# Self-attention of a decoder layer: float32r scores on stacks built inside SBUF, and projections interleaved with the exponentials

## The reference

```python
def attn(x, w_q, w_k, w_v, w_o):                      # 4 batches, 512 tokens, 16 heads of 16
    q, k, v = x @ w_q.T, x @ w_k.T, x @ w_v.T         # reshaped to heads
    scores = einsum('bqhd,bkhd->bhqk', q, k) * 16 ** -0.5
    out = einsum('bhqk,bkhd->bqhd', softmax(scores), v)
    return out.reshape(B, S, 256) @ w_o.T
x = layernorm(x + attn(x, ...))
x = layernorm(x + xattn(x, ctx, ...))                 # the same with keys and values from the context
x = layernorm(x + ffn(x, ...))                        # softmax router, top 2 of 8 experts, exact gelu
```

## Time and profile before

| | us |
|---|---|
| median of 3 runs (885.6 to 890.35) | 889.31 |
| profiled execution | 889.74 |
| its span, first to last instruction | 888.0 |
| front, to the first exp tile | 141 |
| self-attention, to the last PV group | 183.4 |
| the rest | 563.6 |

### The profile page before, as it was taken

How to read it: one execution, slowest core, us unless ns; L and a number is a source line. 1 busy time by engine, 2 the same in 40 slices (tenths; PEclk the granted TensorE clock), 3 DMA queues, 4 the chain that set the end, 5 groups by cost and what they waited for, 6 DMA issues and landing times.

```text
span 888.0 us, 13256 instructions
## 1 busy us (share of the span) xinstructions
PE 686.3 (77%) x4099; PEld 449.1 (51%) x4100; DVE 349.9 (39%) x750; ACT 285.8 (32%) x501; POOL 212.3 (24%) x265
## 2 busy tenths in 40 slices
PE   7572266999999986764677862099999999999980
PEld 3230111322222245541213652089999999999970
DVE  2252344888888546653443875000000000000004
ACT  3220133767666643332354211011111111111112
POOL 1020100111111122112111067213333333333322
PEclk9876786999999999886689995599999999999995
DMA  6999992000001430858713722356666566656615
GB/s 207 129 170 169 141 151 32 3 1 1 1 1 44 136 53 37 134 82 130 98 53 101 250 77 50 105 161 180 175 169 177 167 173 180 174 174 175 170 45 189
DMA packets 75777, 103.61 MB, mean 117 GB/s; under 512 B 15044, under 2 KB 60637, under 8 KB 75742
## 3 DMA queue, kind: packets, MB, share of 16 engines
q1 hardware_dynamic: 63006, 90.53, 45.0%
q0 software_dynamic: 8512, 8.44, 5.8%
q10 hardware_dynamic: 4224, 4.19, 1.7%
HBM read 82.95 MB, written 21.40 MB: 118 GB/s over the span
## 4 chain that ended last, share of the span: by engine, by line
PE 64%; DMA 14%; DVE 7%; SPq 5%; POOL 4%; issue 3%; ACT 2%; DVEq 0%; ACTq 0%; POOLq 0%
PE ps L1566 16%; PE ps L1577 15%; PE ps L1288 7%; DMA scrq<-parts 7%; PE ps L1297 7%; PE ps L1233 5%; SPq L393 3%; POOL metas L664 3%; DMA qst<-mT 3%; PE ps L1381 2%; PE ps L1454 2%; PE ps L1447 2%; DMA qst<-scr_q 1%; PE ps L1413 1%; DVE xr L993 1%
## 5 line engine op out<-in xcount | busy, mean ns | idle before, releaser
L890 DVE TENSOR_REDUCE nmx<-ps 128x1 f32<-128x512 f32 x256 | 160.4, 681 | 55.0 <-PE ps L1233 55.0
L745 ACT ACTIVATE probs<-ps 128x512 f32<-128x512 f32 x256 | 133.8, 606 | 93.7 <-PE ps L1288 93.6
L1566 PEld LDWEIGHTS ps<-xtT,w1c 128*128 128x128 f32 x1248 | 147.1, 194 | 4.3 <-issue 2.4
L1566 PE MATMUL ps<-xtT,w1c 128*128 128x128 f32 x1248 | 147.6, 277 | 1.8 <-ACT xtT L845 1.8
L1577 PE MATMUL ps<-wexp,hidT 128*128 x624 | 141.0, 379 | 0.0
L1198 DVE TENSOR_SCALAR yw<-ps,mt 128x256 f32<-128x256 f32 x39 | 18.9, 484 | 292.2 <-PE ps L1577 292.2
L1577 PEld LDWEIGHTS ps<-wexp,hidT 128*128 128x128 f32 x624 | 115.6, 190 | 14.2
L1288 PE MATMUL ps<-qst,kst 99*128 (+1 forms) x256 | 96.4, 396 | 33.9 <-DMA qst<-mT 31.8
L1233 PE MATMUL ps<-kst,qst 96*128 (+1 forms) x256 | 94.6, 396 | 33.6 <-DVE nmx L890 17.3
L851 ACT ACTIVATE hidT<-ps 128x1024 f32<-128x1024 f32 x39 | 40.0, 1024 | 229.8 <-PE ps L1566 229.8
L703 POOL DMA_INDIRECT acc<-yw,mt x39 | 61.7, 1582 | 172.0 <-DVE yw L1198 172.0
(11 more groups left out here) (162 smaller groups left out, 668.1 us busy)
## 6 DMA issues: line engine op xcount, KB each, us to landing
w1c<-in_w1T SPq DMA_DIRECT2D x39, 1024.0 KB
wexp<-in_w2T SPq DMA_DIRECT2D x8, 1024.0 KB, 5.5
qst<-scrq SPq DMA_DIRECT2D x24, 256.0 KB, 9.2
kst<-scrk SPq DMA_DIRECT2D x24, 256.0 KB, 19.7
qst<-scr_q SPq DMA_DIRECT2D x24, 256.0 KB, 8.8
scrq<-parts SPq DMA_DIRECT2D x4, 768.0 KB, 18.1
scrk<-parts SPq DMA_DIRECT2D x4, 768.0 KB, 18.6
scr_q<-parts SPq DMA_DIRECT2D x4, 768.0 KB, 3.4
```

The lines of the kernel that those rows point to most:

```text
L745: act.activation(probs[n % 8][:, :], ps[:, 4 + n % 3, :], ACT.Exp).then_inc(s_exp, 1)
L890: dve.tensor_reduce(nmx[j % 2][:, k:k + 1], ps[:, slot, :], AX.X, ALU.max, negate=True).then_inc(s_mfree, 1)
L1566: mm = pe.matmul(ps[:, 2 * (j % 2) + f // 4, f % 4 * P:(f % 4 + 1) * P], w1c[j % 2][:, k * FF + f * P:k * FF + (f + 1) * P], xtT[j % 2][:, ...
```

## The change

Scores become float32r matmuls. q and k are split in two parts, high and low, both float32r. Three products (high by high, low by high, high by low) are stacked: 3 x 16 = 48 rows, and two rows for the maximum in two parts, 50 in all. Two heads share the 128 partitions, one at partition 0, one at 64, so consecutive score matmuls alternate between the upper and the lower half of the array. The stacks are double buffers of one batch each (`q_stack`, `k_stack`).

They are filled by DMAs from SBUF to SBUF: for each head and each block one DMA of 16 partitions by 512 float32, 32 KB. That is 24 for one half of q or k of a batch, 96 a batch, 384 in all, issued by SP. The maxima of a unit go in with eight DMAs of 2 KB instead of three of 4 KB. HBM is no longer used for the stacks.

Only batch 0 is projected ahead. The projections of batch b + 1 stand inside the attention of batch b, at exp tiles 5, 12, 23, 33, 41 and 52 of 64, and each is issued in two parts: the first half of its matmuls two exp tiles earlier, after that tile's PV. ACT makes the high part and v, DVE the low part, between exps and maxima. POOL has no part in it any more: the maxima are turned whole by a float32 matmul against the identity (L1222), and DVE splits them. Max tiles run 27 tiles ahead of the exps (LEAD), where they ran 32 ahead, on three banks of PSUM instead of four.

```diff
+UNITS = NB * NU
+TILES = HG * QT
+LEAD = 27
+TURN_AT = 3
+Q_BLOCKS = ("high", "low", "high")
+K_BLOCKS = ("high", "high", "low")
+STACKED = 16 * 2 * len(Q_BLOCKS) * HG
+    NEXT_BATCH_AT = {5: "q0", 12: "k0", 23: "v0", 33: "q1", 41: "k1", 52: "v1"}
...
     @block.sync
-        def make_stacks(b):
-            for qk in range(2):
-                sp.wait_ge(s_p3, 2 * b + qk + 1)
-                sp.dma_start(scr[qk][ds(b, 1)]...).then_inc(s_st[qk], 16)
-            sp.wait_ge(s_stack, 192 * b)
-            for qk, stack, part in ((0, qst, Q_PART), (1, kst, K_PART)):
-                sp.wait_ge(s_st[qk], 16 * (b + 1))
-                for g, r in enumerate(part):
-                    sp.dma_start(stack[HD * g:HD * g + HD, ds(b * H * S, H * S)]...).then_inc(s_stack, 16)
+        def stack(b, n, m):
+            sp.wait_ge(s_high[n], KD * b + m + 1)
+            sp.wait_ge(s_low[n], KD * b + m + 1)
+            for h in range(2 * HG):
+                pair = HG * m + h // 2
+                for g, part in enumerate(Q_BLOCKS if n == "q" else K_BLOCKS):
+                    at = HALF * (h % 2) + HD * g
+                    sp.dma_start((qs, ks)[n == "k"][b % 2][at:at + HD, pair * S:(pair + 1) * S].bitcast(F32),
+                                 staged[f"{n}_{part}", m][HD * h:HD * (h + 1), :].bitcast(F32)).then_inc(s_stack[2 * m + h // HG], 16)
+        def max_rows(w):
+            sp.wait_ge(s_mfree, turn_slot(w) + 1)
+            for r, m in ((TERMS, mT_hi), (TERMS + 1, mT_lo)):
+                for i in range(HG):
...
+        STACKS_BEHIND = {0: ("q", 0), 1: ("k", 0), 2: ("q", 1), 3: ("k", 1)}
+        sp.wait_ge(s_kones[0], 2)
+        for n, m in STACKS_BEHIND.values():
+            stack(0, n, m)
+        for w in range(UNITS):
+            max_rows(w)
+            if w == 0:
+                sp.wait_ge(s_kones[1], 2)
+            if w // NU + 1 < NB:
+                stack(w // NU + 1, *STACKS_BEHIND[w % NU])
+            if w in LOADS_BEHIND:
+                LOADS_BEHIND[w]()
...
     @block.gpsimd
+        for n, at in enumerate((HALF // 2, HALF + HALF // 2)):
+            if n > 0:
+                pool.wait_ge(s_kones[1], n)
+            pool.memset(ks[1][at:at + HALF // 2, :].bitcast(F32), 1.0).then_inc(s_kones[1], 1)
+        pool.wait_ge(s_kones[1], 2)
         pool.memset(pad_v[:, :, 1], 0.0)
         pool.memset(pad_v[:, :, 0].bitcast(I32), NO_TOKEN).then_inc(s_pad, 1)
...
     @block.tensor
+        def exp_tile(e):
+            u, (kt, i) = e // TILES, divmod(e % TILES, HG)
+            if e % TILES == 0:
+                pe.wait_ge(s_mrow[u % 2], 16 * HG * MAX_ROWS * (u // 2 + 1))
+            if e >= 3:
+                pe.wait_ge(s_exp, e - 2)
+            b, pair = u // NU % 2, u % NU * 2 + i // 2
+            rows = slice(HALF * (i % 2), HALF * (i % 2) + TERMS + MAX_ROWS)
...
+        for e in range(UNITS * TILES):
+            exp_tile(e)
+            maxima(e + LEAD)
+            if e % HG == 1 and e >= HG:
+                pv(e // HG - 1)
+            for b, name in projections_at(e + 2):
+                project_begin(b, name)
+            for b, name in projections_at(e):
+                project_end(b, name)
```

More of the change, by code:

```diff
@@ L14 @@
 F32 = mybir.dt.float32
+F32R = mybir.dt.float32r
 BF16 = mybir.dt.bfloat16
@@ L42 @@
 MROWS = ROWS + 3
-M3W = 96
 CAP = T // P
@@ L410, in load_residual @@
         def load_residual(b):
-            sp.wait_ge(s_vu, 2 + NU * (b + 1))
+            if b == 0:
+                for u in range(NU):
+                    sp.wait_ge(s_stack[u], STACKED * NB)
             sl = slice(QT * b, QT * (b + 1))
@@ L740, in exps @@
-        def exps(u):
-            for n in range(HG * QT):
-                act.wait_ge(s_e, HG * QT * u + n + 1)
-                if n % HG == 0 and not (isinstance(u, int) and 4 * u + n // HG < 2):
-                    act.wait_ge(s_pv, 4 * u + n // HG - 1)
-                act.activation(probs[n % 8][:, :], ps[:, 4 + n % 3, :], ACT.Exp).then_inc(s_exp, 1)
-        act.wait_ge(s_proj, 3 * NB)
-        exps(0)
-        with act.Fori(1, NB * NU) as u:
-            exps(u)
+        act.dma_start(xTb[0][:, :].rearrange("p (k n) -> p k n", k=KD),
+                      xT.rearrange("(k p) n -> p k n", p=P)[:, :, 0:S]).then_inc(s_xT[0], 16)
@@ new lines, in evict @@
+        def evict(b, name):
+            {"q": high, "k": high, "v": v_units}[name[0]](b, int(name[1]), name)
+        for name in PROJECTIONS:
+            evict(0, name)
+        for e in range(UNITS * TILES):
+            act.wait_ge(s_e, e + 1)
+            if e % HG == 0 and e >= 8:
+                act.wait_ge(s_pv, e // HG - 1)
+            act.activation(probs[e % 8][:, :], ps[:, 3 + e % 3, :], ACT.Exp).then_inc(s_exp, 1)
+            for b, name in projections_at(e):
+                evict(b, name)
@@ new lines, in max_turn, with maxima @@
+        def max_turn(w):
+            n = turn_slot(w)
+            pe.wait_ge(s_mfree, max(max_slot(w, TILES - 1) + 1, n - 2))
+            pe.matmul(ps[0:TILES, n % 3, 0:P], nmx[w % 2][:, :], identf[:, :], start=True, stop=True).then_inc(s_mready, 1)
+        def maxima(t):
+            w, k = divmod(t, TILES)
+            if w < UNITS:
+                max_tile(w, k)
+            if w > 0 and k == TURN_AT - 1 and w < UNITS:
+                max_turn(w - 1)
+            if t == UNITS * TILES - 1:
+                max_turn(w)
@@ new lines, in pv @@
+        def pv(g):
+            u, kt = divmod(g, QT)
+            b = u // NU
+            if kt == 0:
+                pe.wait_ge(s_oev, u)
+            if u % NU == 0 and kt % 2 == 0:
+                pe.wait_ge(s_vev, 2 * b + kt // 2 + 1)
+            pe.wait_ge(s_exp, HG * (g + 1))
+            for i in range(HG):
+                at = (kt * H + u % NU * HG + i) * VW
+                mm = pe.matmul(ps[VW * i:VW * (i + 1), 7, :], vu[b % 2][:, at:at + VW], probs[g % 2 * HG + i][:, :],
+                               start=(kt == 0), stop=(kt == QT - 1))
+            mm.then_inc(s_pv, 1)
```

504 lines of the change are left out of this document (207 added, 297 removed).

## The result

The changed kernel takes 1019.8 us (1017.01 to 1022.58), the kernel before, measured beside it, 889.24: a ratio of 1.148, 95% interval 1.142 to 1.153. The prediction was 924 us, 868 to 975. It had the direction right, and the size far wrong: 35 us slower was expected, 131 came.

What follows compares the result with a forecast made beforehand. Before: front bound by DMA traffic, attention by PE; after: SP's issue queue. First exp at 65.3 us, plus 244.2 and 48.8, ends attention at 358.3; the untouched 563.6 gives 921.9 span, forecast 924 us, range 868 to 975.

Steps and rivals of the forecast that it cites:

- Step 1: SP's queue: issuing a stack DMA costs 0.49 us, a row DMA 0.60 us.
- SBUF to SBUF issues cost what mT's cost: Rival on SP's queue: 0.60 us a stack issue, attention ends at 400.6, kernel 966 us; no separate chance given.
- Step 2: Kernel start: stacking starts at 12.4 us, after POOL's new memsets and the 1.62 us issue of metas.
- Step 3: Front: the first 96 stack DMAs take 47.0 us, to 59.4; first exp at 65.3 us against 141.1.
- Step 4: Units 0 to 11: SP's issues, loads and waits for q0 and q1 (38.7 us) sum to 244.2 us.
- Step 5: Units 12 to 15, with no stacks behind them: together 48.8 us, so attention ends at 358.3 us.
- Step 6: Splitting each projection in two, two tiles apart: worth nothing under SP's queue, bound 8 us.
- Cheap issues: Rival on SP's queue: 0.36 us a stack issue, attention ends at 305.3, kernel 871 us; 20 in 100.
- engine-bound: Rival in the attention: below 0.29 us an issue, DVE sets 11.9 us a unit, kernel 803 us; 8 in 100.
- slow float32r: Rival in the score matmuls: 0.43 us each gives 944 us, 0.86 to 0.9 some 1,180; 4 in 100.

## Why the prediction was wrong

**What bounds the kernel.** Right. The queue was named as the one late, with a unit of 20 us and PE, DVE and ACT hidden behind it, and runs with more issues and with fewer moved the time as that says. The unit took 26.2 us on average, though. What was foretold of the trace came: holes of PE released by the row DMAs, a low DMA share (0.17), a falling clock.

**Step 1, the price of an issue: wrong, and the largest error.** 384 x (0.632 - 0.49) is 55 of 100 us. The step's reason was "by the row that also writes 16 partitions of a stack in a long burst". It matched shape and burst, and left out where the data come from, though the row that had the new operation's two memories and its count of pieces, SBUF to SBUF in 16 pieces, stood beside it at 0.60 (its DMAs are smaller, 4 KB on one partition). I said so in the rival "SBUF to SBUF issues cost what mT's cost" and called 966 us the slow end of my own case. With 0.632 in my own formula the attention ends at 170.2 + 242.7 = 412.9, and the kernel at 978: just outside the range with this term alone.

**Step 2, the start**: stacking began 1.5 us earlier than predicted; the issue of metas took 0.36 us and not 1.62.

**Step 3**: 47.0 against 61.0, the price again.

**Step 4, the waits for own projections: 38.7 against 60.3.** The places and their number were right, and they count in full. I took the durations in them from rows at clock 0.98, and wrote in its last part that the clock falls at just these holes. What the low clock costs was seen and not put into the sum. Work on PE in its holes gave 13 of the 21.6 us back.

**Step 5, units 12 to 15: 48.8 against 65.9.** In the kernel with q1 early, whose clock in these units was 0.97 on average, they take 57.7: 13.0, 14.3, 11.8 and 18.6 where the sum had 11.8, 11.8, 9.8 and 15.4. So some 9 us are an error of my count near full clock. Part of it is in the maxima of the next unit: its row DMAs began 7.0 and 8.3 us after the first exp tile of units 12 and 13, and the sum had 5.9. The other 8 go with the clock, as far as two runs can tell. Unit 12 and unit 13 of the changed kernel:

```profile
393.00:406.00 13.00, 11.02 (x66) 3.98 (x66) 11.04 (x19) 8.45 (x16) 0.00 (x0) 1.00 0.14 43
406.00:422.00 16.00, 15.84 (x66) 5.41 (x66) 10.21 (x18) 7.74 (x15) 0.00 (x0) 0.57 0.11 35
```

The same 66 matmuls take 13 us at full clock and 16 at 0.57, where PE is busy nearly all the time. The prediction said that the engines need 11 to 12 us; at the low clock PE is the bound.

**Step 6, the parts**: worth nothing, right, in both kernels.

**The rivals.** Cheap issues and engine-bound are out: in bursts on SP the median stack issue took 0.632 us and never under 0.55, the median row issue 0.62, and both rivals need less than 0.40. A slow float32r is out as well. In unit 12 of the changed kernel, at full clock, a pair on the two halves moves on after 0.23 us here, 0.34 elsewhere, and two bf16 matmuls took 0.44:

```profile
395.01 0.39 PE L1275 MATMUL ps<-q_stack,k_stack 50*128 50x512 f32 x1
395.01 0.62 PE L1216 MATMUL ps<-k_stack,q_stack 48*128 48x512 f32 x2
395.24 0.39 PE L1275 MATMUL ps<-q_stack,k_stack 50*128 50x512 f32 x1
```

The Trainium skill, "DMA: Bandwidth & Descriptors", section "Issuing engines are not separate DMA queues", has it that starting DMAs from several engines only saves the sequencer's time, and that this is usually small. The first half agrees with the runs here. The second does not: in units 0 to 11 the DMA share was 0.17, and the sequencer's time, 242 us of stack and row issues, set the pace of 315. Moving half of the stack issues to another engine, with the order mended, took 159 us off.

**The range** ended at 975. It held the price to 0.60, the dearest row, and had nothing for the waits and the last units, which together added 39 us. Some 21 of these are the low clock (13 in the waits, 8 in the last units), and they come on the same side as the price, since a late queue is what makes the holes that lower the clock.

## What to carry to other kernels

A DMA's issue is priced by the row whose source and destination lie in the same memories, before shape or size. Here SBUF to SBUF cost 0.632 us where HBM to SBUF cost 0.463, and hundreds of them on one queue made the path. When the sum says that a queue starves PE, the terms that contain PE work must be taken at the low clock's durations as well, and the range must grow on that side. And before adding issues to a queue, write down what stands behind each wait in it: a second queue gave 102 us, and the order of two calls in it another 57 (62 by the ratios).

## What was not expected of the hardware

- SP's issue of a 32 KB DMA from SBUF to SBUF costs 0.632 us start to start in 16 pieces and 0.652 in 256, from HBM to SBUF 0.463. A load from HBM right behind an SBUF to SBUF issue is dear as well: `xwo_s` took 0.58 there and 0.42 behind loads from HBM. POOL's issue of the same SBUF to SBUF DMA costs 0.475, and both queues ran at once.
- Busy PE alone did not bring the clock back: in the kernel with LEAD 26 it stood at 0.50 for units 12 and 13 with PE busy for 38.6 of 38.6 us. Matmuls of the same shapes, with LEAD 27, ran at 0.99 in the kernel without the later stacks. Which of the last units run at the low clock differs between kernels whose last units have the same program, and what decides it stays open.
- Float32r score matmuls of 50 and 48 rows on opposite halves of the array start together (409.04 in the changed kernel), and by the trace's records PE starts one ahead of another that stands before it in the program when that one's half is taken (415.17 and 415.77 in the kernel with LEAD 26).
